# A graph layer and a feed-forward layer in one kernel: the stages of a node block spread over four rounds instead of two

## The reference, cut to what matters

```python
def reference(x, src, dst, edge_type, rel_w, h_bias, loop_w, wr, br, w1, b1, w2, b2):
    n = layernorm(x)
    msg = einsum('ni,rio->rno', n, rel_w)[edge_type, src]
    g = x + segment_sum(msg, dst, 6250) * 0.5**0.5 + h_bias + (n @ loop_w) * 0.5**0.5
    m = layernorm(g)
    w = m @ wr + br
    y = (gelu(m @ w1 + b1) @ w2 + b2) * w
    # the 3124 nodes of largest w get y added, the others do not
    return g + m + where(selected(w), y, 0)
```

## Time and profile before

| what | us |
|---|---|
| median of 3 runs | 2652.16 (2643.42 to 2662.25) |
| profiled execution | 2643.06 |
| its span, first to last instruction | 2641.1 |
| busy: PE / PEld / POOL / DVE / ACT | 1862.2 / 1656.9 / 1621.1 / 943.1 / 581.9 |
| granted TensorE clock, mean | 0.863 |

### The profile page before, as it was taken

How to read it: one execution, slowest core, us unless ns; L and a number is a source line. 1 busy time by engine, 2 the same in 40 slices (tenths; PEclk the granted TensorE clock), 3 DMA queues, 4 the chain that set the end, 5 groups by cost and what they waited for, 6 DMA issues and landing times.

```text
span 2641.1 us, 39380 instructions
## 1 busy us (share of the span) xinstructions
PE 1862.2 (71%) x10848; PEld 1656.9 (63%) x10849; DVE 943.1 (36%) x1937; ACT 581.9 (22%) x852; POOL 1621.1 (61%) x1641
## 2 busy tenths in 40 slices
PE   1257777678777787777767777777776777778781
PEld 1147676667667676666666666666675767667671
DVE  6123333233333333333333333333333333333336
ACT  5111221122122131131213112122111212113130
POOL 2766666666666666666666666666666666666500
PEclk9568898888889888888888989889888988888995
DMA  7523333333333333333333333333333333333305
GB/s 254 151 83 94 95 97 95 89 96 97 97 93 95 100 94 92 95 94 94 95 93 91 94 96 95 95 93 96 99 92 95 96 100 93 92 96 97 88 31 172
DMA packets 126206, 264.48 MB, mean 100 GB/s; under 512 B 30131, under 2 KB 71435, under 8 KB 126175
## 3 DMA queue, kind: packets, MB, share of 16 engines
q0 software_dynamic: 79264, 218.32, 28.8%
q1 hardware_dynamic: 46911, 45.83, 5.4%
HBM read 244.79 MB, written 19.25 MB: 100 GB/s over the span
## 4 chain that ended last, share of the span: by engine, by line
another core or an unknown queue 38%; PE 19%; issue 17%; ACT 10%; DVE 7%; DVEq 6%; DMA 1%; ACTq 1%; SPq 0%; POOL 0%; POOLq 0%
PE bank L645 7%; PE bank L625 6%; PE bank L673 4%; ACT hidden L519 2%; DVEq L933 2%; ACT L519 2%; DVE sums L944 2%; ACT sums L504 2%; ACT closed L498 2%; ACT L498 1%; DVEq L944 1%; PE bank L648 1%; DVE stats L971 1%; DVE x L968 1%
## 5 line engine op out<-in xcount | busy, mean ns | idle before, releaser
L393 POOL DMA_INDIRECT messages<-normed_table,gather_rows x1616 | 1607.1, 994 | 878.7 <-issue 419.2
L625 PE MATMUL bank<-onehot,messages 128*128 128x128 f32 x6464 | 898.4, 301 | 103.1 <-issue 86.2
L625 PEld LDWEIGHTS bank<-onehot,messages 128*128 128x128 f32 x6464 | 870.8, 216 | 128.3 <-issue 119.5
L944 DVE SCALAR_TENSOR_TENSOR sums<-bank,regular,sums 128x256 f32 x808 | 391.0, 484 | 1358.4 <-remote 738.7
L645 PE MATMUL bank<-rel_sb,closed 128*128 128x256 f32 x1568 | 405.7, 397 | 114.9 <-issue 106.9
L664 PE MATMUL bank<-normed_t,w_sb 128*128 128x128 f32 x1568 | 301.1, 342 | 225.8 <-issue 168.9
L645 PEld LDWEIGHTS bank<-rel_sb,closed 128*128 128x128 f32 x1568 | 300.8, 197 | 203.9 <-issue 160.5
L664 PEld LDWEIGHTS bank<-normed_t,w_sb 128*128 128x128 f32 x1568 | 261.9, 247 | 263.1 <-issue 262.6
L861 DVE TENSOR_TENSOR onehot<-iota,keys 128x1024 f32<-128x1024 f32 x203 | 248.9, 1226 | 135.5 <-issue 111.2
L673 PE MATMUL bank<-w_sb,hidden 128*128 128x256 f32 x784 | 203.6, 418 | 85.0 <-ACT hidden L519 82.7
L673 PEld LDWEIGHTS bank<-w_sb,hidden 128*128 128x128 f32 x784 | 160.2, 210 | 118.5 <-issue 94.5
(11 more groups left out here) (149 smaller groups left out, 497.2 us busy)
## 6 DMA issues: line engine op xcount, KB each, us to landing
messages<-normed_table,gather_rows POOLq DMA_INDIRECT x1616
normed_x<-normed_table SPq DMA_DIRECT2D x49, 128.0 KB
residual<-resid SPq DMA_DIRECT2D x49, 128.0 KB
x_block<-in_x SPq DMA_DIRECT2D x48, 128.0 KB
node_out<-acc SPq DMA_DIRECT2D x12, 512.0 KB
messages<-in_x POOLq DMA_DIRECT2D x6, 896.0 KB, 16.8
normed_table<-messages SPq DMA_DIRECT2D x6, 896.0 KB, 8.5
messages<-residual SPq DMA_DIRECT2D x6, 896.0 KB, 10.9
```

The lines of the kernel that those rows point to most:

```text
L393: pool.indirect_dma_start(messages[0:EP, g % RING, j * D:(j + 1) * D], None, table, bass.IndirectOffsetOnAxis(ap=gather_rows[0:EP, g, j:j ...
L625: last = nc.tensor.matmul(banks[u][:, h * D + k * P:h * D + (k + 1) * P], messages[0:EP, slot, j * D + k * P:j * D + (k + 1) * P], onehot[ ...
L944: V.scalar_tensor_tensor(sums[:, :, bass.ds(to[h], W)], banks[u][:, h * D:(h + 1) * D].rearrange("p (n m) -> p n m", m=W), regular[:, 0:1] ...
```

## The change

Everything of a block that followed its sums is spread over four rounds. `PIPE` goes from 2 to 3, so there is one drain round more, and `round_code` holds a fourth bit: **rises**. `ffn_turn` stays in round i+1 but now stands behind sum 3. `ffn_first` and the gelu go to round i+2, between sums 1 and 2 (ACT: behind the close). `ffn_second` and `ffn_leave` go to round i+3, behind sum 0 and in the same place on DVE as before. `loop_turn` stands behind sum 2 instead of sum 1 and uses bank 7, so it waits for `ffn_done` of the block that left last; the wait for `agg_taken` moves to `relation_products`. On ACT `sums` is cleared before `normed_x_t` is copied.

```diff
-    PIPE = 2
+    PIPE = 3
...
             def close(b):
...
                 nc.scalar.activation(closed[:, :, :], sums[:, :, bass.ds(slot, P)], ACT.Copy).then_inc(closed_ready, 1)
-                act.wait_ge(loop_turned, b + 1)
-                nc.scalar.activation(normed_x_t..., banks[4][:, 0:D], ACT.Copy).then_inc(loop_t_ready, 1)
                 act.wait_ge(closed_ready, b + 1)
                 act.sem_inc(wait_carrier, 1)
                 nc.scalar.activation(sums[:, :, bass.ds(slot, OPEN)], zero...).then_inc(slot_cleared, 1)
+                act.wait_ge(loop_turned, b + 1)
+                nc.scalar.activation(normed_x_t..., banks[7][:, 0:D], ACT.Copy).then_inc(loop_t_ready, 1)
...
                 with act.If(enters > 0):
                     close(blocks[0])
+                with act.If(rises > 0):
+                    ffn_activate(blocks[2])
                 with act.If(follows > 0):
                     ffn_deviate_and_turn(blocks[1])
-                    ffn_activate(blocks[1])
...
-            def loop_turn(b):
+            def loop_turn(b, left):
                 pe.wait_ge(normed_x_in, 16 * b + 16)
-                pe.wait_ge(agg_taken, b + 1)
+                pe.wait_ge(ffn_done, 2 * left + 1)
...
             def relation_products(b):
                 pe.wait_ge(closed_ready, b + 1)
                 pe.wait_ge(loop_t_ready, b + 1)
+                pe.wait_ge(agg_taken, b + 1)
...
                 sum_one(0)
                 with pe.If(leaves > 0):
-                    ffn_second(blocks[2])
+                    ffn_second(blocks[3])
                 sum_one(1)
+                with pe.If(rises > 0):
+                    ffn_first(blocks[2])
+                sum_one(2)
                 with pe.If(enters > 0):
-                    loop_turn(blocks[0])
-                sum_one(2)
+                    loop_turn(blocks[0], blocks[2])
+                sum_one(3)
                 with pe.If(follows > 0):
                     ffn_turn(blocks[1])
-                sum_one(3)
-                with pe.If(follows > 0):
-                    ffn_first(blocks[1])
                 with pe.If(enters > 0):
                     relation_products(blocks[0])
```

More of the change, by code:

```diff
@@ L114, in gnn_ffn_program @@
             flat[0:1, 11 * GP * BANK + k * BANK // 2:11 * GP * BANK + k * BANK // 2 + n]
-            for k, n in enumerate((STEPS, STEPS, STEPS, STEPS, STEPS + 3)))
+            for k, n in enumerate((STEPS, STEPS, STEPS, STEPS, STEPS + PIPE + 1)))
         ring_rows = messages[:, :, :].rearrange("p s (v d) -> p (s v) d", d=D)
@@ L498, in close @@
                 nc.scalar.activation(closed[:, :, :], sums[:, :, bass.ds(slot, P)], ACT.Copy).then_inc(closed_ready, 1)
-                act.wait_ge(loop_turned, b + 1)
-                nc.scalar.activation(normed_x_t[:, :, :].rearrange("p k n -> p (k n)"), banks[4][:, 0:D],
-                                     ACT.Copy).then_inc(loop_t_ready, 1)
                 act.wait_ge(closed_ready, b + 1)
@@ L505, in close @@
                                      ACT.Copy).then_inc(slot_cleared, 1)
+                act.wait_ge(loop_turned, b + 1)
+                nc.scalar.activation(normed_x_t[:, :, :].rearrange("p k n -> p (k n)"), banks[7][:, 0:D],
+                                     ACT.Copy).then_inc(loop_t_ready, 1)
             def ffn_deviate_and_turn(b):
@@ L807, in order_stage @@
                 row(V.tensor_tensor_scan(highest_goal, goal, steps_goal, 0.0, ALU.max, ALU.max))
-                row(V.memset(entered[:, 0:3], 0.0))
-                row(V.tensor_tensor_scan(entered[:, 3:3 + STEPS], steps_one, highest_goal, 0.0, ALU.add, ALU.min))
-                e = [entered[:, n:n + STEPS] for n in range(4)]
-                row(V.tensor_scalar(steps_goal, e[2], float(FIELD), None, ALU.mult))
-                row(V.scalar_tensor_tensor(steps_goal, e[3], float(FIELD), steps_goal, ALU.mult, ALU.add))
-                row(V.scalar_tensor_tensor(steps_goal, e[1], float(2 * FIELD), steps_goal, ALU.mult, ALU.add))
-                row(V.scalar_tensor_tensor(round_code[:, :], e[0], float(1 - 4 * FIELD), steps_goal, ALU.mult, ALU.add))
-                row(V.tensor_scalar(many_left_i[:, :], entered[:, 3 + ROUNDS + DRAIN - 3:3 + ROUNDS + DRAIN - 2], float(NB), None, ALU.is_lt))
+                row(V.memset(entered[:, 0:PIPE + 1], 0.0))
+                row(V.tensor_tensor_scan(entered[:, PIPE + 1:PIPE + 1 + STEPS], steps_one, highest_goal, 0.0, ALU.add, ALU.min))
+                e = [entered[:, n:n + STEPS] for n in range(PIPE + 2)]
+                row(V.tensor_scalar(steps_goal, e[3], float(FIELD), None, ALU.mult))
+                row(V.scalar_tensor_tensor(steps_goal, e[4], float(FIELD), steps_goal, ALU.mult, ALU.add))
+                row(V.scalar_tensor_tensor(steps_goal, e[2], float(2 * FIELD), steps_goal, ALU.mult, ALU.add))
+                row(V.scalar_tensor_tensor(steps_goal, e[1], float(4 * FIELD), steps_goal, ALU.mult, ALU.add))
+                row(V.scalar_tensor_tensor(round_code[:, :], e[0], float(1 - 8 * FIELD), steps_goal, ALU.mult, ALU.add))
+                row(V.tensor_scalar(many_left_i[:, :], entered[:, PIPE + 1 + ROUNDS:PIPE + 2 + ROUNDS], float(NB), None, ALU.is_lt))
                 by_round = [a[:, 0, 0:NG].rearrange("p (i u) -> p i u", u=SLOTS) for a in (lowest, highest)]
-                past, now = (entered[:, 2 + n:2 + n + ROUNDS].unsqueeze(2) for n in range(2))
+                past, now = (entered[:, PIPE + n:PIPE + n + ROUNDS].unsqueeze(2) for n in range(2))
                 row(V.tensor_copy(by_round[0][:, :, 0:1], past))
@@ L999, in finish_round @@
             def finish_round(i, add_one, all_added, wait_cleared):
-                (enters, follows, leaves), blocks, entered_after = phases(dve, i)
+                (enters, follows, _, leaves), blocks, entered_after = phases(dve, i)
                 add_one(0)
```

17 lines of the change are left out of this document (9 added, 8 removed).

## The result

The changed kernel takes 2681.39 us (median of 4 runs, 2680.14 to 2685.12) against 2649.11 for the kernel before (4 runs); the ratio is 1.0107, 95% interval 1.0082 to 1.0131. It is 1.1% slower. Forecast were 2578 and 2.8% faster. The profiled execution after took 2685.12 us, its span is 2683.1.

The account below looks back on a forecast made before the run. Rounds were taken to last as long as POOL's 16 issues plus its waits for PE (403.1 us). 2643.1 - 67 - 6 = 2570, about 2578 for the median; own range 2530 to 2612, 8 in 10: 2490 to 2665.

Parts of the forecast that it names:

- Kind one: POOL's wait for sum 1 of the even round, PE late through ffn_second's gelu wait: would go, -67 us net.
- The -77: POOL's wait for sum 1 of the even round gone: mean 1.6 us times 48 rounds, before 10 us coming back.
- Kind two: POOL's waits for sums 3 and 0, seen late while POOL issues: taken as 0 change, bounds nothing and 250 us.
- the first rival: All late sums go: every sum seen before POOL asks; its sign was POOL's waits for sum 3 gone; chance 0.15.
- no change: POOL's wait only moves, since it must pause 5 to 6 times a pair for PE's semaphores: 2630 to 2650; chance 0.18.
- All late sums go: POOL's late sums vanish with PE nearly a round ahead: median 2454 if half go, 2321 if all; chance 0.15 together.
- Slower: ACT hears of ffn_turn late, delaying ffn_first, relation products and sum 0: +210 us, or half, about 2755; chance 0.12.
- ffn_first, loop_turn: 0: Moved behind sums 1 and 2, covered by POOL's issues: 0 each; bounds 48 us and 0 to 3 us a pair.
- Tail, -6: After 2499.5, PE's waits of 3.22, 0.55 and 2.35 us fall away: -6 us, bounds 0 and 12.
- ACT 0: On ACT, three table loads a block as before and the clearing 0.4 us earlier, off POOL's path: 0.

Follow-up runs that it names:

- e11: Kernel before with only ffn_second and ffn_leave a round later, behind sum 0 of the odd round; late call: 2671.99 us against 2640.13, ratio 1.0114.
- e16: Kernel before with ffn_second behind sum 1 instead of sum 0 of the even round, ffn_leave behind sum 2's addition; late call: 2611.39 us against 2648.11, 0.9855.
- e17: Kernel before with one-hot build by tensor_scalar and ffn_second behind sum 1 of the even round; late call: 2633.89 us against 2648.11, 0.9946.
- e15: Kernel before with most relation products, half of ffn_first and 6 of 8 of ffn_second left out; late call: 2608.91 us against 2652.74, 0.9827.
- e6: Kernel before, unaltered, profiled in a prompt call: 2307.80 us.
- e7: Kernel before with DVE's one-hot build as eight tensor_scalar instead of one tensor_tensor, keys in float32; prompt call: 2217.27 us against 2311.33, 0.9602.

## Why the prediction was wrong

**What bounds the kernel.** "The rounds last as long as POOL's issues and its waits for PE" is true as a sum and was the wrong thing to build on. It gives the time by itself in prompt calls, where the waits are nil. In a late call a change at one place moves issues and waits at others. Busy, waits and own gaps of POOL against the late profile of before: after -29.8, +47.0, +13.1; e11 -9.4, +30.7, +5.8; e16 +31.0, -79.9, +19.0; e17 -61.9, +35.2, +12.5. I took the waits as a cost that can be struck out one by one. Over the whole run they stand as follows, in us by the sum that POOL waits for (the first issue of each group; a round is even where PE's relation products stand in it; waits under 0.4 us left out):

| waits for | before | after | e11 | e16 |
|---|---|---|---|---|
| sum 0, even | 56.7 | 104.3 | 141.7 | 71.0 |
| sum 1, even | 74.5 | 8.9 | 0.8 | 5.3 |
| sum 2, even | 7.8 | 100.1 | 66.5 | 100.1 |
| sum 3, even | 90.1 | 8.2 | 31.6 | 0.5 |
| sum 0, odd | 60.0 | 139.3 | 74.7 | 45.0 |
| sum 1, odd | 5.2 | 57.4 | 57.3 | 35.6 |
| sum 2, odd | 10.2 | 9.7 | 10.1 | 20.7 |
| sum 3, odd | 98.2 | 24.1 | 48.1 | 44.2 |

**Kind one, -67 us: the step that failed.** The wait for the gelu did end, and nearly all waiting for sum 1 of the even round with it (74.5 us, then 8.9). What failed is "Does it come back in the odd round? ... I leave 0.2 us a pair, 10 us; bounds 0 and 34". It came back: sum 1 of the odd round went from 5.2 to 57.4 us of waits, and to 57.3 in e11, 52 us more in 39 and 40 more waits, so 40 us net of POOL's own 0.30 each, beyond the bound of 34. The -77 was too much as well. It was read from two waits and taken times 48; over the run there were 43 waits, 74.5 us, of which 0.30 each is POOL's own, so 61.6. And the waits at other sums did not stand still: e11, in which ffn_second and ffn_leave alone go to the odd round, pays 30.7 us more in waits than before, over 100 us more than e16 in the same regime.

That e16's 79.9 us lie near the 77 is chance. There too the wait came back, behind the stage's new place: sum 1 of the even round fell by 69.2 and sum 2 rose by 92.3. What it gained came from sum 3, 143.6 us less over both rounds, a term that the forecast had at 0, and of the 79.9 only 37 reached the time. So the place of the same stage decides the sign, by all the waits that shift with it and not by the wait struck out. In e11 and e16 ffn_leave moved on DVE together with ffn_second on PE; neither was moved alone.

**Kind two, "unchanged": wrong in kind.** The waits for sum 3 nearly went (188.3 to 32.3 us over both rounds), those for sum 0 doubled (116.7 to 243.6) and those for sum 2 of the even round came up (7.8 to 100.1). Together this is 63 us more where 0 stood, and more than the whole loss in waits. The sign set down for the first rival, waits for sum 3 gone, thus showed without its gain. The sign for "no change", waits of 1 us and more at sum 1 of the odd and sum 2 of the even round, showed in 42 and 43 waits, of 1.4 and 2.3 us on average. Its reason, that POOL must pause some times in a pair for PE's news whatever PE does, is borne out only in part: with PE's stages cut down 355.7 us of waits remain (e15), but the order of the stages moves the total between 323.2 and 450.1. That rival had 0.18.

**All late sums go** had its chance of 0.15 for the wrong reason. No edit run in a late call makes them go; in four of the nine calls behind the first measurement they aren't there, and the kernel before then takes 2310, close to the "2312 or 2321" worked out for that floor. The rule weighed there (the Trainium skill, SBUF — State Buffer, Who interferes with whom: DMA never contends with a compute engine, PE waits on nobody) agrees with the prompt calls, where the same gathers delay nothing. In the late ones PE's records are held up while gathers are in flight (23 in 55 us), and the rule does not account for it; what holds them, no run here shows.

**Slower.** Its sign and two of its marks came: ACT's copy starts 9.6 us after ffn_turn's records in the median over the 49 blocks (3.75 before), and POOL's waits for sum 0 reach 2.76 and 3.00 us. They are not needed as the cause: e11 has none of its moved parts, its copy starts 1.4 us after the turn, and it loses as much.

**ffn_first, loop_turn: 0.** Not tested singly in a late call. after and e11 lie at +1.07% and +1.14%, so what they add up to is small; a gain and a loss among them can hide each other.

**Tail, -6.** It came out 12.4 us longer (from the last gather's end 153.0 instead of 140.6). 3.1 us are PE's backlog at the last round's sum 0. The last block's stages take the rest. In the trace of after the relation products wait for the copy of normed_x_t, which now stands behind the clearing of 2.12 us; the gelu's table is no longer loaded ahead; and ffn_second takes 6.77 us for its 16 records where it took 3.72 before (granted clock 0.54 in this stretch, 1.00 before):

```profile
2587.76 2.12 ACT L502 ACTIVATE sums<-zero 128x2304 f32 x1
2589.79 0.36 ACT L505 ACTIVATE normed_x_t<-bank 128x256 f32<-128x256 f32 x1
...
2590.25 10.08 PE L648 MATMUL bank<-rel_sb,closed 128*128 128x256 f32 x32 [8.93 <-issue]
...
2610.28 1.28 ACT L520 ACT_TABLE_LOAD   x1 [4.91 <-PE bank L667]
...
2613.89 6.77 PE L676 MATMUL bank<-w_sb,hidden 128*128 128x256 f32 x16 [3.71 <-ACT hidden L520]
```

I counted only waits between rounds there, and "ACT 0" held for the rounds, not for the last block. In prompt calls the two tails are alike (108.3 and 109.0).

**What stays open.** What makes a call late; why PE's news mostly comes through when POOL pauses; and why ffn_second and ffn_leave in the odd round draw longer pauses than in the even one. The runs show that they do, not why.

## What to carry to other kernels

A wait on the pacing engine is worth what is left when the same work stands elsewhere: take the wait away with the least move (here one sum later in the same round, -1.45% in one late call and -0.5% in a prompt one) before spreading stages over more rounds. Where news between engines comes late in the trace, ask first whether the same program shows it in another call; what was read from waits in one regime says nothing where these waits are absent. And look at the longest instances of the pacing instruction, not only at its waits: 99 us lay in gather issues that began while a long two-input DVE operation ran.

## What the runs showed of the hardware that I had not expected

- The same program takes 2310 or 2650 us by the call. In the late kind PE's records come singly, mostly 2.1 to 3.5 us apart at the start, while gathers are in flight (23 in 55 us against 179), and POOL waits 403 us for it; after the last gather ffn_turn is seen 0.1 us after its records.
- A gather issue of POOL takes 0.95 us. Begun while a DVE tensor_tensor of 1024 columns with both inputs in SBUF runs, it ends 0.82 us after that instruction (144 of 148 in e6); begun just before it, it takes 0.95. In e7, where eight tensor_scalar stand in its place, the mean is 0.95.
- In a late call, issues 92.9 us shorter came with 115.1 us more of waits (e17 against e16).
